# Two attention blocks and a routed feed-forward: LayerNorm statistics for the group three ahead, and its shifts on GpSimd

## What is computed

```
m = mean(x); v = var(x); xn = (x - m) / sqrt(v + 1e-5)      # per row

# first block: causal linear attention, 16 heads of 8
q, k = f(xn @ wq + bq), f(xn @ wk + bk);  v = xn @ wv + bv   # f(y) = y + 1 if y > 0 else exp(y)
S, z = running sums over the rows of a sequence of k v^T and k
x = x + (q S / (q z + 1e-6)) @ wo + bo

# second block: autocorrelation with a context (only its Gram matrices are formed in the stage spoken of here)
# third block: two of eight experts per row
```

## Time and profile before

| what | value |
|---|---|
| three runs | 624.18, 625.54, 626.89 us; median 625.54 |
| the profiled execution, its own time | 626.32 us |
| its span, first to last instruction | 624.1 us |
| busy share: TensorE, VectorE, ScalarE, GpSimd | 89%, 81%, 67%, 65% |
| attention stage | 0 to about 270 us |

### The profile page before, as it was taken

How to read it: one execution, slowest core, us unless ns; L and a number is a source line. 1 busy time by engine, 2 the same in 40 slices (tenths; PEclk the granted TensorE clock), 3 DMA queues, 4 the chain that set the end, 5 groups by cost and what they waited for, 6 DMA issues and landing times.

```text
span 624.1 us, 16569 instructions
## 1 busy us (share of the span) xinstructions
PE 556.2 (89%) x4286; PEld 407.8 (65%) x4287; DVE 504.1 (81%) x1506; ACT 417.6 (67%) x1188; POOL 407.6 (65%) x459
## 2 busy tenths in 40 slices
PE   4888999999999998878899786899999999999993
PEld 1333444444444444445888544799999999999993
DVE  4489999999999999874578988466887878877883
ACT  3556878888888775532888502445887888878882
POOL 2778888888888888112877501764566766757762
PEclk9979999999999999899999969999999999999998
DMA  5510111111161112362568480221111111111110
GB/s 153 187 50 2 35 35 36 35 34 34 34 101 34 34 37 65 67 137 57 159 196 206 78 137 5 59 51 38 35 50 51 47 44 47 52 40 51 52 45 22
DMA packets 49973, 40.99 MB, mean 66 GB/s; under 512 B 21971, under 2 KB 40278, under 8 KB 49926
## 3 DMA queue, kind: packets, MB, share of 16 engines
q1 hardware_dynamic: 44150, 29.68, 19.5%
q0 software_dynamic: 4960, 10.49, 6.4%
q10 hardware_dynamic: 816, 0.26, 0.2%
HBM read 27.54 MB, written 12.88 MB: 65 GB/s over the span
## 4 chain that ended last, share of the span: by engine, by line
PE 55%; ACT 16%; DVE 10%; issue 10%; POOL 4%; DMA 3%; ACTq 0%; SPq 0%; DVEq 0%; POOLq 0%
PE bank L1349 30%; PE run L1349 19%; ACT xh L678 4%; PE bank L1353 4%; ACT xs L780 2%; ACT ex L656 2%; DMA shared<-xs_d,row_u 2%; ACT nb_a L675 2%; PE run L1616 1%; ACT ex L661 1%; DVE mean_early L1057 1%; ACT xT L649 1%; PE run L1540 1%; DMA ct<-in_ctx_r 1%; ACT rl L657 1%
## 5 line engine op out<-in xcount | busy, mean ns | idle before, releaser
L616 POOL DMA_INDIRECT shared<-xs_d,row_u x91 | 87.8, 965 | 62.6 <-DVE row_u L1247 31.6
L549 POOL TENSOR_TENSOR shared<-v,qk 128x1024 f32<-128x1024 f32 x64 | 125.0, 1953 | 2.8
L623 POOL DMA_INDIRECT out_x<-shared x64 | 63.5, 992 | 48.2 <-DVE shared L1319 22.1
L899 DVE TENSOR_TENSOR R<-run,qk 128x1024 f32<-128x1024 f32 x64 | 77.5, 1210 | 12.5 <-PE run L1349 11.0
L1349 PE MATMUL bank<-wqkv,xT 128*64 128x128 f32 (+1 forms) x384 | 70.5, 353 | 15.5 <-ACT v L659 10.8
L1349 PEld LDWEIGHTS bank<-wqkv,xT 128*64 128x64 f32 (+1 forms) x384 | 33.4, 159 | 72.1 <-issue 37.4
L909 DVE TENSOR_REDUCE num<-R 128x128 f32<-128x1024 f32 x64 | 77.2, 1206 | 1.1
L1349 PE MATMUL run<-shared,tris_s 64*64 64x512 f32 x512 | 73.3, 644 | 0.0
L809 ACT ACTIVATE shared<-run,scale_s 128x128 f32<-128x128 f32 (+1 forms) x78 | 30.0, 385 | 41.5 <-PE run L1616 41.5
L540 POOL TENSOR_TENSOR qk<-ex,rl 128x256 f32<-128x256 f32 x64 | 46.5, 727 | 11.0 <-DVE mv_a L884 7.5
L656 ACT ACTIVATE ex<-bank 128x256 f32<-128x256 f32 x64 | 24.1, 376 | 28.9 <-PE bank L1349 28.9
(11 more groups left out here) (277 smaller groups left out, 1425.1 us busy)
## 6 DMA issues: line engine op xcount, KB each, us to landing
xs_d<-xs SPq DMA_DIRECT2D x16, 270.0 KB, 5.2
X<-in_x SPq DMA_DIRECT2D x16, 256.0 KB, 2.7
ct<-in_ctx_t SPq DMA_DIRECT2D x16, 256.0 KB, 3.0
ct<-in_ctx_r SPq DMA_DIRECT2D x16, 256.0 KB, 3.7
gram_d<-gd SPq DMA_DIRECT2D x14, 256.0 KB, 2.4
w_s<-in_w_experts SPq DMA_DIRECT2D x8, 384.0 KB, 3.9
circ<-prob_d SPq DMA_DIRECT2D x30, 64.0 KB, 2.8
shared<-xs_d,row_u POOLq DMA_INDIRECT x91, 2.6
```

The lines of the kernel that those rows point to most:

```text
L549: nc.gpsimd.tensor_tensor(outer[k].rearrange("p (h e d) -> p h e d", h=H, e=D), vv.unsqueeze(3).broadcast_to([P, H, D, D]), kk.unsqueeze(2 ...
L616: nc.gpsimd.indirect_dma_start(xg[q], None, xs_d[:, :], bass.IndirectOffsetOnAxis(ap=rows, axis=0)).then_inc(xg_in[q], 16)
L623: nc.gpsimd.indirect_dma_start(out[:, :], bass.IndirectOffsetOnAxis(ap=xg[(NXI + j) % NX][:, DEST:DEST + 1].bitcast(U32), axis=0), yg[q], ...
L899: nc.vector.tensor_tensor(R[:, 0:D * E].rearrange("p (h e d) -> p h e d", h=H, e=D), run[k % 2][:].rearrange("p (h e d) -> p h e d", h=H, ...
```

## The change

- `slots`: one more slot at the front (FIRST is -3), and the loop covers slots 4 to 11 in place of 4 to 13; the last slots are written out.
- VectorE: `stats` and `moments` of the input are for the group three ahead (z, n+3), and stand around `key_dots`. X is added behind the third `sum_heads` (k = 2) in place of before it; the statistics of c stand behind the fourth `times_q`, their moments behind the fourth `sum_heads`. In `last_rows` the two instructions for the shift go.
- GpSimd: `variance` and `root` of z stand later in the slot; new are `mean_times_root` (mean * rs, 128x4) and `shift` (nb = 1 - that, 128x4), for z in the same slot, and for the second normalisation at the start of the slot after its root.
- ScalarE: `negative_mean` and the 128x1 activations go. The 128x128 activations stay where they were, for the same groups.

```diff
-        FIRST, LAST = -2, NG + 1
+        FIRST, LAST = -3, NG + 1
...
-            with eng.Fori(2, (NG - 2) // 2) as i:
+            with eng.Fori(2, (NG - 4) // 2) as i:
...
# GpSimd
+            def mean_times_root(g, p, mv, rs, rs_sem, mr, mr_sem, nb_sem):
+
+                pool.wait_ge(rs_sem, g + 1)
+                need(pool, nb_sem, g)
+                nc.gpsimd.tensor_tensor(mr[:], mv[p][:, :, 0], rs[p][:], ALU.mult).then_inc(mr_sem, 1)
+
+            def shift(g, p, mr, mr_sem, nb, nb_sem, normed):
+
+                pool.wait_ge(mr_sem, g + 1)
+                need(pool, normed, GT * (g - 1))
+                settle(pool)
+                nc.gpsimd.tensor_scalar(nb[p][:], mr[:], -1.0, 1.0, ALU.mult, ALU.add).then_inc(nb_sem, 1)
...
# ScalarE
-            def norm(g, p, rs, rs_sem, mr, mr_sem, nb, nb_sem, dst, dst_sem, own=GT):
-                act.wait_ge(rs_sem, g + 1)
-                act.wait_ge(mr_sem, g + 1)
+            def norm(g, p, rs, nb, nb_sem, dst, dst_sem, own=GT):
+                act.wait_ge(nb_sem, g + 1)
                 for k in range(own):
-                    nc.scalar.activation(nb[p][:, k:k + 1], mr[:, k:k + 1], ACT.Copy, bias=1.0, scale=rs[p][:, k:k + 1]).then_inc(nb_sem, 1)
-                for k in range(own):
-                    act.wait_ge(nb_sem, GT * g + k + 1)
...
# VectorE
                 if c:
                     quotients(*c)
+                if z:
+                    g, p, r = z
+                    dve.wait_ge(x_in[p], 16 * r + 16)
+                    stats(g, p, st_a, a_st, mv_a, a_mv, a_mr, 1)
                 if b:
                     key_dots(*b)
-                if a0:
-                    g, p, r = a0
-                    dve.wait_ge(x_in[p], 16 * r + 16)
-                    stats(g, p, st_a, a_st, mv_a, a_mv, a_nb, GT)
+                if z:
+                    moments(z[0], z[1], st_a, a_st, mv_a, a_mv, a_mr, 1)
                 if b:
                     sum_heads(*b, 1)
                     sum_dots(*b)
-                if a0:
-                    moments(a0[0], a0[1], st_a, a_st, mv_a, a_mv, a_nb, GT)
...
                 if b:
                     times_q(*b, 2)
+                    sum_heads(*b, 2)
                 if c:
                     add_attention(*c)
                 if b:
-                    sum_heads(*b, 2)
+                    times_q(*b, 3)
                 if c:
                     dve.wait_ge(c_x1, c[0] + 1)
-                    stats(c[0], c[1], st_c, c_st, mv_c, c_mv, c_nb, GT)
-                if b:
-                    times_q(*b, 3)
-                if c:
-                    moments(c[0], c[1], st_c, c_st, mv_c, c_mv, c_nb, GT)
+                    stats(c[0], c[1], st_c, c_st, mv_c, c_mv, c_mr, 1)
                 if b:
                     sum_heads(*b, 3)
+                if c:
+                    moments(c[0], c[1], st_c, c_st, mv_c, c_mv, c_mr, 1)
```

More of the change, by code:

```diff
@@ L146, in build @@
         xh2 = sb("xh2", [P, GT, E])
-        last_mr = sb("last_mr", [P, GT // 2])
         x2T, k2T = sb("x2T", [P, GW]), sb("k2T", [P, GW])
@@ L319, in slots @@
                 slot(n, None)
-            with eng.Fori(2, (NG - 2) // 2) as i:
+            with eng.Fori(2, (NG - 4) // 2) as i:
                 slot(0, i)
                 slot(1, i)
-            for n in range(NG - 2, LAST + 1):
+            for n in range(NG - 4, LAST + 1):
                 slot(n, None)
@@ L553, in slot @@
             def slot(n, i):
-                a0, a1, c = stage(n, i, 2), stage(n, i, 1), stage(n, i, -1)
-                of_a = a0 and (a0[0], a0[1], mv_a, a_mv, ve_a, a_ve, rs_a, a_rs, a_xh)
+                z, a1, c, d = (stage(n, i, k) for k in (3, 1, -1, -2))
+                of_z = z and (z[0], z[1], mv_a, a_mv, ve_a, a_ve, rs_a, a_rs, a_xh)
                 of_c = c and (c[0], c[1], mv_c, c_mv, ve_c, c_ve, rs_c, c_rs, d_xh)
@@ L560, in slot @@
                     features(*a1, 0)
-                if a0:
-                    variance(*of_a)
+                if d:
+                    mean_times_root(d[0], d[1], mv_c, rs_c, c_rs, mr_c, c_mr, c_nb)
+                    shift(d[0], d[1], mr_c, c_mr, nb_c, c_nb, d_xh)
                 if a1:
@@ L565, in slot @@
                     features(*a1, 1)
-                if a0:
-                    root(*of_a)
-                if a1:
                     outer_product(*a1, 1)
                     features(*a1, 2)
+                if z:
+                    variance(*of_z)
+                if a1:
+                    outer_product(*a1, 2)
+                if z:
+                    root(*of_z)
+                if a1:
+                    features(*a1, 3)
+                if z:
+                    mean_times_root(z[0], z[1], mv_a, rs_a, a_rs, mr_a, a_mr, a_nb)
                 if c:
                     variance(*of_c)
+                if z:
+                    shift(z[0], z[1], mr_a, a_mr, nb_a, a_nb, a_xh)
                 if a1:
-                    outer_product(*a1, 2)
-                    features(*a1, 3)
+                    outer_product(*a1, 3)
                 if c:
                     root(*of_c)
-                if a1:
-                    outer_product(*a1, 3)
             slots(pool, slot)
@@ L690, in slot @@
                     a_evac_xT(*a1)
-                if d:
-                    negative_mean(d[0], d[1], mv_c, c_mv, mr_c, c_mr)
                 if a1:
@@ L703, in slot @@
                     need(act, d_tr, g)
-                    norm(g, p, rs_c, c_rs, mr_c, c_mr, nb_c, c_nb, xh2, d_xh, GT // 2 if i is None and g == NG - 1 else GT)
+                    norm(g, p, rs_c, nb_c, c_nb, xh2, d_xh, GT // 2 if i is None and g == NG - 1 else GT)
                 if d:
@@ L717, in slot @@
                     need(act, a_tr, g)
-                    negative_mean(g, p, mv_a, a_mv, mr_a, a_mr)
-                    norm(g, p, rs_a, a_rs, mr_a, a_mr, nb_a, a_nb, xh, a_xh)
+                    norm(g, p, rs_a, nb_a, a_nb, xh, a_xh)
                 if a1:
@@ L965, in slot @@
             def slot(n, i):
-                a0, a1, b, c = (stage(n, i, s) for s in (2, 1, 0, -1))
+                z, b, c = (stage(n, i, k) for k in (3, 0, -1))
                 if b:
@@ L986, in slot @@
                     sum_dots(*b)
-                if a0:
-                    moments(a0[0], a0[1], st_a, a_st, mv_a, a_mv, a_nb, GT)
-                if i is None and n == FIRST:
+                if i is None and n == -3:
                     fold_projection()
@@ L1031, in last_rows @@
             def last_rows(g, p):
[L1032 to L1038, removed]
+                dve.wait_ge(c_nb, g + 1)
                 dve.wait_ge(d_tr, g)
```

7 lines of the change are left out of this document (2 added, 5 removed).

## The result

| | before | after |
|---|---|---|
| median | 625.44 us (624.18 to 626.89, 4 runs) | 619.22 us (618.95 to 620.20, 4 runs) |
| the profiled execution, own time | 626.32 us | 619.28 us |
| its span | 624.1 us | 617.4 us |
| ratio, 95% interval | | 0.9899, 0.9867 to 0.9932 |

The change makes the kernel 1.0% faster. In the trace the gain is complete when the attention stage ends: the reduction behind it (mean_early, itself 7.1 us long) starts at 269.74 us before and at 262.63 after, 7.1 us earlier. Of these, 0.4 us are lost again in the blocks behind, going by the spans (624.1 and 617.4 us).

What follows compares the result with a forecast made beforehand. VectorE was nearest full (96%), with a chain through ScalarE in slots of 14.83 us. Ten slots -3.6, slots 1 to 3 -1.6, start -2.1, tail 0: -7.3 us, 619.0, as median 618.2; stated 618.6, range 614.8 to 622.8.

Steps and rivals of the forecast that it cites:

- start, reciprocal of slot 1: Attention stage's start: VectorE reaches slot 1's reciprocal at 37.9 us in place of 39.98, -2.1 us.
- three slots from 1 to 4: Slots 1 to 3: VectorE bounds the first two at about 14.3, then 14.47; 43.1 in place of 44.7, -1.6 us.
- tail, slot 14 to mean_early: Slots 15 to 17: two more GpSimd instructions (0.5) replace ScalarE's two and VectorE's two (0.3); 0, within 0.5 us.
- GpSimd's own slot: GpSimd per slot: 13.17 us of work plus four 128x4 instructions and a dependent pair, 14.27 us in all.
- VectorE's own slot: VectorE alone would need 14.4 us a slot; the bounds put the slot's floor at its 14.3.
- The lower bound: Lowest time for the whole kernel: 13 slots at 0.5 and the start give -9.5 us, and 616.
- the ten small instructions: ScalarE per slot: only mr_a and four nb_a count, xh starts 1.07 us earlier; TensorE's own loop falls to 14.0.
- The loop: From TensorE's last running sums through VectorE to the transposes of `on` and back: it decides the slot at 14.47 us.
- the third rival: GpSimd becomes the bound: added instructions cost 0.32 us each in place of 0.22, slot 14.7, time 623; chance 0.09.
- the fifth: Slower: the four small GpSimd instructions take 0.45 us each, GpSimd's slot is 15.4, time 633; chance 0.04.
- The fourth rival: Shift of the second normalisation is late, ScalarE waits, nothing gained in the slot: 623 to 625; chance 0.08.
- The second rival: Clock falls again at the start, TensorE's key sums waiting for slot 0's last features: -4, time 622; chance 0.14.

Runs made afterwards that it cites:

- X early: Changed kernel with X added before the third sum again and the statistics of c before the fourth product: 618.52 us, ratio 0.9868.
- both edits: Changed kernel with X before the third sum again and the second normalisation's root as a multiplication in place of a power: 618.27 us, ratio 0.9848.
- one more instruction: Changed kernel with one more 128x4 multiplication per slot on GpSimd, result not used: 621.72 us, ratio 0.9935.
- the new order: Changed kernel with X before the third sum and GpSimd's small instructions spread so none follows the one it waits for: 617.90 us, ratio 0.9861.
- the cheap root: Changed kernel with the second normalisation's root on GpSimd as a multiplication in place of a power: 619.77 us, ratio 0.9873.

## Why the prediction was right

The median was to be 618.6 us, in a range of 614.8 to 622.8; it is 619.22. Term by term, each in the profiled execution (GpSimd's and VectorE's own pace in the looped slots):

| term | on record | measured |
|---|---|---|
| start, reciprocal of slot 1 | 37.9 | 37.96 |
| three slots from 1 to 4 | 43.1 | 43.16 |
| slots 4 to 14, each | 14.47 | 14.42 |
| tail, slot 14 to mean_early | 0, within 0.5 | +0.6 |
| behind the stage | 0 | +0.4 |
| GpSimd's own slot | 14.27 | 14.45 |
| VectorE's own slot | 14.3 to 14.4 | 14.32 (X early) |

The mechanism was right, and so was each place of the gain. That the total fits so well is in part luck. Up to slot 14 the gain is 7.7 us in place of 7.3, the tail and the blocks behind lose 1.0 us that stood at nothing, and the execution's own time fell by 0.3 us more than its span. The sum on record gives 618.2 us, and the step from there to 618.6 has no working. The lower bound's -9.5 us doesn't follow from its terms either (13 slots at 0.5 and a start of 2.1 give 8.6).

- **ScalarE.** What the record shows is that the ten small instructions together are worth the two waits of TensorE, for xT and xh: putting them back brought both waits and 0.39 us a slot. That only the five before xh count was not tested by itself. For it speaks that ScalarE now waits before x2T (0.38 us in the slot shown, 0.49 on average), though I had expected 0.9. The 0.39 us before the third projection stand, as said.
- **The loop.** The experiments bear it out: relief on GpSimd gave nothing, a shorter loop gave 0.10 us. The slot was 0.05 us shorter than its sum. The two handovers, both estimates, came out at 0.06 in place of 0.16 and at 0.15 in place of 0.05, and these errors cancel (in the slot shown, which took 14.46). The prediction gives the loop's growth as 0.78 us and, a few lines on, as 0.6; by its rows it is 0.6, since the last sum, with the moments behind it, holds VectorE for 1.13 us in place of 1.32.
- **GpSimd.** This is the term that was mis-sized, by 0.18 us a slot. I had counted 0.28 us from mean times root to shift; it was 0.42 to 0.48. Features to the outer product behind it took 0.97 to 1.07 in place of 0.81 in the looped slots. So GpSimd was not "under the loop by 0.2" but 0.03 over it, and it didn't show because GpSimd started with a lead. The small instructions took 0.19 and 0.20 us each, as in the rows; neither the third rival (0.32) nor the fifth (0.45) came about. Its waits came to 0.49 us a slot, where under 0.4 was to be the sign of being right.
- **The fourth rival** came true in small. ScalarE waits for the shift of the second normalisation in seven of the ten slots, up to 0.4 us at a time, which was on record as a sign of being wrong. It stayed inside what ScalarE had to spare before x2T.
- **The start.** The stop of GpSimd and the wait of VectorE at 37.58 went together. With the statistics three groups ahead and the shifts on GpSimd or ScalarE the reciprocal of slot 1 stands at 37.5 to 38.3 in every profile; with two groups, in any of the three kernels that have it, at 39.9 to 40.1. With the shifts on VectorE the gain is lost for another reason, a first product that starts 6.8 us later.
- **The second rival** came true too, in its mechanism, and cheaply. TensorE's key sums do wait for the last features of slot 0, in both profiles of the changed kernel alike:

```profile
39.12 1.13 PE L1349 MATMUL bank<-qk,tris_s 128*128 128x256 f32 x4 [2.34 <-POOL qk L551]
```
```profile
39.05 2.07 PE L1349 MATMUL bank<-qk,tris_s 128*128 128x256 f32 x4 [2.33 <-POOL qk L551]
```

In the first the granted clock stayed at 2.4 GHz; in the second it was at 1.2 GHz from 38.5 to 41.9 us, and the reciprocal of slot 2 came at 52.81 in place of 52.14. Of these 0.67 us, 0.20 stood already at slot 1, before the clock fell, so the stretch cost about 0.5. I had priced this rival at 3.3 us, more than the whole start. The clock also fell there with X back, with both edits, with one more instruction and with the new order, and not with the cheap root: that the first profile of the changed kernel was without it is luck.

- **The tail.** Slot 14 to slot 16 took the same time in both. From there to mean_early it is 10.17 us in place of 9.51: VectorE waits 1.48 us for nb_c, which now comes through two more GpSimd instructions and the gaps before them (before, it waited 0.68 us for rs_c and formed the shift itself), and its two parts of xh2 then take 0.82 us from 261.81 on in place of 0.52. I had counted 0.2 for this, and 0.5 at most.

What I left out: moving X late was not worth its wait. I had weighed the change as one, and had not asked what the rest would give without it.

## What to carry to other kernels

When engines pass work round in a pipeline of slots, lay out the loops that go through several engines before believing the busiest engine's own bound: here VectorE, busy for 96% of the time, gave up only what the loop let it. Read the pace of each engine slot by slot and not as a mean: an engine that is too slow by 0.1 us a slot can hide behind its lead for seven slots, and a mean then shows room that isn't there. An instruction whose input arrives too late in the slot costs twice, its own time and the stop behind which all the engine's other work queues; take its input one group further ahead first, and only then give that engine more to do. Where one engine does two tiny dependent instructions, put an independent one between them: here that took GpSimd's waits in ten slots from 4.9 us to 1.9 (without those for other engines), though no total shows it. And try each part of a change without the others: one part of this one cost time.

## What the runs showed of the hardware

VectorE's small product with both inputs in SBUF waits for GpSimd. With the shifts on VectorE, mr_c took 851 ns on average over 16, mr_a right behind it 144 ns, for the same work (in the groups of the trace; x16 is the count, then busy us, mean ns, idle before):

```profile
L876 DVE TENSOR_TENSOR mr_c<-mv_c,rs_c 128x4 f32<-128x4 f32 x16 | 13.6, 851 | 1.8 <-POOL rs_c L529 1.8
L883 DVE TENSOR_SCALAR nb_c<-mr_c 128x4 f32<-128x4 f32 x16 | 8.1, 506 | 2.6 <-issue 1.5 <-DVE mr_c L876 0.8
L883 DVE TENSOR_SCALAR nb_a<-mr_a 128x4 f32<-128x4 f32 x16 | 4.7, 291 | 0.8 <-DVE mr_a L876 0.7
L876 DVE TENSOR_TENSOR mr_a<-mv_a,rs_a 128x4 f32<-128x4 f32 x16 | 2.3, 144 | 0.0
```

Twelve of the sixteen mr_c took 0.5 to 1.8 us, and each of the twelve ended within 0.02 us of the end of an outer product on GpSimd; the other four took 0.12 to 0.16, three of them beside no GpSimd instruction and one beside a memset, which reads nothing. The shifts were held up too: the nb_c at 147.92, above, took 0.44 us and ended 0.03 us behind GpSimd's features (147.60 to 148.33). The large instructions of VectorE in this stage have at most one input in SBUF (the products take the other from PSUM, the sums have only R), and all 64 of each kind take 1.18 to 1.23 us, in the kernel before, the changed one and this one, however busy GpSimd is. The Trainium skill (SBUF — State Buffer, Who interferes with whom) states this: an instruction of VectorE with two SBUF inputs, or a tensor_scalar in a mode with two ports, contends with a GpSimd instruction that reads SBUF, and the second to come is blocked until the first has ended. The trace agrees, in 1.16 us for a product of 0.15.

The other rule of the Trainium skill, the one that I had weighed against the change (GPSIMD Engine Reference, Engine selection), has the direction right for the product by itself: undisturbed, one of this size takes 0.12 to 0.16 us on VectorE and 0.20 on GpSimd, though that is less than the factor of about two. And yet moving the four there cost 27.6 us (647.8 against 620.2, in other sessions; the ratios are 1.0376 and 0.9904). Of this some 9 us lie before the reciprocal of slot 1 and 1.67 us in each slot. What makes it so dear, as far as the trace shows, is that the instructions stand between `on` and the sums, on the engine that is busiest, beside one that computes 80% of the time here.
